# A decoder layer's front stage: the projection on B, C and the step size in two fp32r passes, and another order of the second loop

## What is computed

```
xz = layernorm(x) * gamma + beta  @ W_in          # 256 -> 2 x 512
x_inner, z = split(xz)
x_conv = silu(conv1d(x_inner, conv_w, 4 taps) + conv_b)
xp = x_conv @ W_x                                 # 512 -> 16 (B) + 16 (C) + 1 (step)
Bmat, Cmat, delta = xp[:16], xp[16:32], softplus(xp[32])
h = exp(delta * A) * h + delta * B * x_conv       # along the tokens
y = (sum_n h * C + x_conv * D_skip) * silu(z)
x = layernorm(x + (y @ W_out + x))
```

## Time and profile before

| | us |
|---|---|
| median of 3 runs | 1918.02 (1914.12 to 1920.33) |
| the profiled execution, its own time | 1918.45 |
| its span | 1916.7 |
| TensorE busy in the span | 1763.7 (92%) |
| VectorE, ScalarE, GpSimd busy | 1075.5, 757.1, 709.6 |
| first loop | about 17 to 278 us of the span |
| second loop | about 290 to 558 us |
| the stages behind it (attention, experts) | about 569 us to the end |

### The profile page before, as it was taken

One profiled execution on the slowest core, in us unless ns is written; L12 is line 12 of the kernel. 1 busy time (PEld: TensorE's weight loads), 2 busy tenths in 40 slices (PEclk: granted clock), 3 DMA queues, 4 the chain that ended last, 5 costly groups with the idle time before them and its releaser, 6 DMA issues.

```text
span 1916.7 us, 33397 instructions
## 1 busy us (share of the span) xinstructions
PE 1763.7 (92%) x8984; PEld 1440.8 (75%) x8985; DVE 1075.5 (56%) x2536; ACT 757.1 (40%) x1355; POOL 709.6 (37%) x623
## 2 busy tenths in 40 slices
PE   6999987999947899999999998999999999999980
PEld 4666655888845778888888876888888888888870
DVE  6777767888825567666676773333333333333326
ACT  5777754666512332322323232332333333333326
POOL 1110005898822334534445352332332232232233
PEclk9999998999977899999999999999999999999995
DMA  4444465888624332122221244333333333333329
GB/s 135 171 170 170 170 225 155 244 263 251 234 78 147 101 104 91 69 73 90 79 90 68 76 156 122 54 52 53 52 53 53 51 54 54 51 54 52 52 36 353
DMA packets 137704, 220.63 MB, mean 115 GB/s; under 512 B 40544, under 2 KB 110368, under 8 KB 129328
## 3 DMA queue, kind: packets, MB, share of 16 engines
q1 hardware_dynamic: 112064, 184.44, 29.1%
q0 software_dynamic: 25584, 35.54, 10.8%
HBM read 122.79 MB, written 97.12 MB: 115 GB/s over the span
## 4 chain that ended last, share of the span: by engine, by line
PE 39%; DMA 11%; POOL 6%; issue 6%; DVE 4%; ACT 2%; SPq 1%; POOLq 0%; ACTq 0%; DVEq 0%
PE back_ps L2381 13%; DMA acc<-back_y,back_token 9%; PE back_ps L2401 8%; PE back_ps L2283 5%; POOL back_turned_qk L1663 4%; PE back_ps L2269 3%; POOL sorted L1651 3%; PE back_ps L2260 3%; PE back_ps L2390 2%; PE back_ps L2214 2%; ACT back_out L1816 2%; PE back_ps L2222 2%; DVE back_y L2136 1%; DMA back_c_raw<-in_ctx_T 1%; PE back_ps L2369 1%
## 5 line engine op out<-in xcount | busy, mean ns | idle before, releaser
L2381 PE MATMUL back_ps<-back_w_gu,back_xe_T 128*128 x1620 | 407.6, 400 | 0.3 <-issue 0.2
L1689 POOL DMA_INDIRECT acc<-back_y,back_token x135 | 210.1, 1556 | 499.4 <-DVE back_y L2136 456.0
L2381 PEld LDWEIGHTS back_ps<-back_w_gu,back_xe_T 128*128 128x128 f32 x1620 | 295.4, 189 | 58.7 <-issue 1.0
L2129 DVE TENSOR_TENSOR back_h<-back_silu,back_ps 128x512 f32<-128x512 f32 x135 | 92.7, 687 | 366.9 <-PE back_ps L2381 366.9
L2401 PE MATMUL back_ps<-back_w_down,back_he_T 128*128 x1080 | 255.6, 380 | 0.8 <-ACT back_he_T L1810 0.8
L2401 PEld LDWEIGHTS back_ps<-back_w_down,back_he_T 128*128 128x128 f32 x1080 | 195.1, 191 | 21.6 <-issue 1.0
L1147 PE MATMUL front_ps<-front_xn_T,front_w_in_parts 128*128 128x512 f32 x768 | 186.4, 399 | 5.2 <-issue 3.3
L1651 POOL DMA_INDIRECT sorted<-back_x,back_slot x128 | 133.7, 1044 | 134.8 <-DVE back_slot L1960 100.6
L1147 PEld LDWEIGHTS front_ps<-front_xn_T,front_w_in_parts 128*128 128x128 f32 x768 | 143.3, 190 | 48.3 <-issue 18.5
L993 DVE SCALAR_TENSOR_TENSOR front_conv<-front_ps,front_conv_wb,front_conv 128x508 f32<-128x508 f32 (+2 forms) x192 | 141.2, 742 | 63.3 <-ACT front_conv L829 58.8
L1810 ACT ACTIVATE back_he_T<-back_ps 128x512 f32<-128x512 f32 x135 | 80.7, 598 | 242.4 <-PE back_ps L2390 242.4
(11 more groups left out here) (222 smaller groups left out, 2892.7 us busy)
## 6 DMA issues: line engine op xcount, KB each, us to landing
back_xe<-sorted SPq DMA_DIRECT2D x135, 136.0 KB, 2.1
gate_T<-front_gate_T SPq DMA_DIRECT2D x16, 1024.0 KB, 4.7
xc_T<-front_xc_T SPq DMA_DIRECT2D x16, 1024.0 KB, 5.6
front_xc_in<-xc_T SPq DMA_DIRECT2D x16, 1024.0 KB, 5.4
front_gate_in<-gate_T SPq DMA_DIRECT2D x16, 1024.0 KB, 6.4
front_x_rows<-in_x SPq DMA_DIRECT2D x16, 512.0 KB, 5.4
front_c_rep<-c_parts SPq DMA_DIRECT2D x128, 64.0 KB, 4.5
front_rows_in<-in_x SPq DMA_DIRECT2D x16, 512.0 KB, 7.3
```

The costliest lines, as they stand in the source:

```text
L1689: pool.indirect_dma_start(out=d["acc"][:, :], out_offset=bass.IndirectOffsetOnAxis(ap=token[:, r:r + 1], axis=0), in_=y[:, r % 2], in_offs ...
L2381: op = nc.tensor.matmul(dst[:, r % 2], xe_T[:, r % 2, x_part, k], w_gu[:, bass.ds(e, 1), m, w_part, k], start=(n == 0), stop=(n == len(PAS ...
```

## The change

1. **First loop.** `project_xp` no longer multiplies `w_x` in full fp32. `split_w_x` (VectorE, once) puts high part and rest of `w_x` side by side in `w_x_parts` (97 columns). For each j, ScalarE rounds `xc_T` (`round_xc`), GpSimd takes the rest (`rest_of_xc`), and TensorE multiplies the 97 columns by both parts: two fp32r passes per j, in four places of the body instead of one. The rows 64 to 96 of the result are copied out by ScalarE (`evacuate_xp`, now ahead of `evacuate_turned`) and added by VectorE (`join_xp`, ahead of `split`). `evacuate_xp_rows` comes later.
2. **Between the loops.** The last group's `join_xp` stands inside the first `softplus`; the second `softplus` comes before the second loop; the step sizes too are split into high part and rest (`delta_parts`).
3. **Second loop.** `late` and `early` are two fp32r passes each, on masks made twice (16 small ScalarE instructions a step instead of 8). VectorE: first two skip terms, the statistics of k-2, last two skip terms, then the products. GpSimd: gates in two halves round the norm, `inner` scaled one step ahead (`scale_segment`). ScalarE: first two `dx` ahead of the masks, exp of `inner` one step ahead, at the step's end.

The diff, cut to its core:

```diff
+            def rest_of_xc(g, u, j):
+                pool.wait_ge(xc_high_ready, KI * g + j + 1)
+                nc.gpsimd.tensor_tensor(xc_parts[:, j % 2, 1], xc_T[:, u, j], xc_parts[:, j % 2, 0].bitcast(F32),
+                                        ALU.subtract).then_inc(xc_low_ready, 1)
...
+                    if not is_at(g, 0):
+                        rest_of_xc(g - 1, 1 - u, KI - 1)
+                    rest_of_xc(g, u, 0)
+                    rest_of_xc(g, u, 1)
                     if not last:
-                        rstd_of(2 * pair + u + 2, u)
+                        rstd_of(g + 2, u)
+                    rest_of_xc(g, u, 2)
...
+            def apply_gate(k, u, first):
+                if first == 0:
+                    pool.wait_ge(gate_loaded[u], loads(k, u))
+                for j in (first, first + 1):
+                    pool.wait_ge(skip_added, KI * k + j + 1)
+                    nc.gpsimd.tensor_tensor(y_T[:, u, j], y_T[:, u, j], gate_in[:, u, j], ALU.mult).then_inc(y_ready, 1)
...
+                if there(k):
+                    apply_gate(k, u, 0)
...
+                    apply_gate(k, u, 2)
+                if there(k + 2):
+                    scale_segment(k + 2)
...
+            def round_xc(g, u, j):
+                act.wait_ge(xc_ready, KI * g + j + 1)
+                if not (is_at(g, 0) and j < 2):
+                    act.wait_ge(xp_part_done, KI * g + j - 1)
+                nc.scalar.activation(xc_parts[:, j % 2, 0], xc_T[:, u, j], ACT.Copy).then_inc(xc_high_ready, 1)
+
+            def evacuate_xp(g):
+                act.wait_ge(xp_part_done, KI * (g + 1))
+                if not is_at(g, 0):
+                    act.wait_ge(xp_T_ready, g)
+                nc.scalar.activation(xp_low, ps_xp[XP_LOW:XP_BOTH], ACT.Copy).then_inc(xp_low_ready, 1)
...
                     bias_tap(g, u, 1)
                     silu_conv(g, u, 0)
                     gate(g, u, 1)
+                    round_xc(g, u, 0)
+                    if not is_at(g, 0):
+                        evacuate_xp(g - 1)
                     if ahead:
                         evacuate_turned(g + 1)
-                    if not is_at(g, 0):
-                        evacuate_xp(g - 1, 1 - u)
                     bias_tap(g, u, 2)
                     silu_conv(g, u, 1)
                     gate(g, u, 2)
+                    round_xc(g, u, 1)
+                    bias_tap(g, u, 3)
+                    silu_conv(g, u, 2)
                     if not is_at(g, 0):
                         evacuate_xp_rows(g - 1)
-                    bias_tap(g, u, 3)
-                    silu_conv(g, u, 2)
                     gate(g, u, 3)
+                    round_xc(g, u, 2)
...
+                act.wait_ge(delta_parts_ready, 4 if is_at(g, GROUPS - 1) else 2)
+                act.sem_inc(act_passed, 1)
+                for part in range(2):
+                    for s in range(GS):
+                        step_size = delta_parts[:, part].bitcast(F32)[:, bass.ds(g * GS + s, 1)]
+                        nc.scalar.activation(upto[:, part, s], masks[:, MASK_UPTO], ACT.Copy, scale=step_size
+                                             ).then_inc(upto_ready, 1)
+                        nc.scalar.activation(after[:, part, s], masks[:, MASK_AFTER], ACT.Copy, scale=step_size
+                                             ).then_inc(after_ready, 1)
...
+                    if not early_group(g):
+                        act.wait_ge(y_done, KI * (g - 1))
+                    scale_x(g, ug, 0)
...
+                if there(k + 2):
+                    act.wait_ge(scaled, k + 3)
+                    nc.scalar.activation(inner, inner, ACT.Exp).then_inc(inner_exp, 1)
...
+            def split_w_x():
+                gap = XP_LOW - XP
+                nc.vector.tensor_copy(w_x_parts[:, :, 0:XP], w_x).then_inc(w_x_ready, 1)
+                nc.vector.tensor_copy(w_x_parts[:, :, XP:XP_LOW], w_x[:, :, 0:gap]).then_inc(w_x_ready, 1)
+                dve.wait_ge(w_x_ready, 1)
+                nc.vector.tensor_tensor(w_x_parts[:, :, XP_LOW:], w_x, w_x_parts[:, :, 0:XP].bitcast(F32),
+                                        ALU.subtract).then_inc(w_x_ready, 1)
+
+            def join_xp(g, u):
+                dve.wait_ge(xp_low_ready, g + 1)
+                dve.wait_ge(xp_stored[u], loads(g, u, 32) - 16)
+                if not early_group(g):
+                    dve.wait_ge(xp_turned, g - 1)
+                nc.vector.tensor_tensor(xp_T[:, u], ps_xp[0:XP], xp_low, ALU.add).then_inc(xp_T_ready, 1)
...
                     convolve(g, u, 1)
+                    if not is_at(g, 0):
+                        join_xp(g - 1, 1 - u)
                     if not (last and u):
                         split(g + 1, 1 - u)
...
+                if a == 0:
+                    join_xp(GROUPS - 1, 1)
...
+            softplus(most, SEQS)
+            all_steps(most, SEQS)
             choose()
...
+                    add_skip(k, u, 0)
+                if there(k - 2):
+                    g = k - 2
+                    for s in range(GS):
+                        dve.wait_ge(sum_ready, 2 * g + s // 2 + 1)
+                        nc.vector.bn_stats(stats_1[:, s], sum_rows[:, s]).then_inc(stats_1_ready, 1)
+                    dve.wait_ge(stats_1_ready, GS * (g + 1))
+                    dve.sem_inc(dve_passed, 1)
+                    for s in range(GS):
+                        nc.vector.bn_aggr(mean_1[:, s], stats_1[:, s]).then_inc(mean_1_ready, 1)
+                if there(k):
+                    add_skip(k, u, 2)
...
+            def project_xp(g, j):
+                pe.wait_ge(xc_low_ready, KI * g + j + 1)
+                if is_at(g, 0) and j == 0:
+                    pe.wait_ge(w_x_ready, 3)
+                elif j == 0:
                     pe.wait_ge(xp_T_ready, g)
-                for j in range(KI):
-                    pe.wait_ge(xc_ready, KI * g + j + 1)
-                    op = nc.tensor.matmul(ps_xp, w_x[:, j], xc_T[:, u, j], start=(j == 0), stop=(j == KI - 1))
-                op.then_inc(xp_done, 1)
+                for part in range(2):
+                    op = nc.tensor.matmul(ps_xp, w_x_parts[:, j], xc_parts[:, j % 2, part], start=(j == 0 and part == 0),
+                                          stop=(j == KI - 1 and part == 1))
+                op.then_inc(xp_part_done, 1)
...
                     project(g, u, 0)
+                    if not is_at(g, 0):
+                        project_xp(g - 1, 2)
                     project(g, u, 1)
+                    if not is_at(g, 0):
+                        project_xp(g - 1, 3)
                     if not (last and u):
                         turn(g + 1, 1 - u)
-                    if not is_at(g, 0):
-                        project_xp(g - 1, 1 - u)
                     project(g, u, 2)
-                    if not is_at(g, 0):
-                        turn_xp(g - 1, 1 - u)
-                    project(g, u, 3)
+                    project_xp(g, 0)
+                    project(g, u, 3, None if is_at(g, 0) else lambda: turn_xp(g - 1, 1 - u))
+                    project_xp(g, 1)
...
+                    pe.wait_ge(upto_ready, 2 * GS * (g + 1))
+                    for part in range(2):
+                        op = nc.tensor.matmul(ps_late, mask_ends[:, 0], upto[:, part].rearrange("p s t -> p (s t)"),
+                                              start=(part == 0), stop=(part == 1))
+                    op.then_inc(late_done, 1)
                     if not is_at(g, 0):
                         pe.wait_ge(products_ready, g)
-                    pe.wait_ge(after_ready, GS * (g + 1))
-                    nc.tensor.matmul(ps_early, masks[:, MASK_EARLY], after.rearrange("p s t -> p (s t)"), start=True,
-                                     stop=True).then_inc(early_done, 1)
+                    pe.wait_ge(after_ready, 2 * GS * (g + 1))
+                    for part in range(2):
+                        op = nc.tensor.matmul(ps_early, mask_ends[:, 1], after[:, part].rearrange("p s t -> p (s t)"),
+                                              start=(part == 0), stop=(part == 1))
+                    op.then_inc(early_done, 1)
```

140 lines of the change are left out of this document (69 added, 71 removed).

## The result

The kernel after takes 1923.72 us (median of 20 runs, 1921.07 to 1927.02) where the kernel before takes 1918.69 beside it (20 runs, 1914.12 to 1921.53): a ratio of 1.0029, 95% interval 1.0023 to 1.0035. That is 5 us slower, inside my range of 1893 to 1928, but to the other side of 1918 than my 1915. The execution profiled took 1923.97 us, 5.5 more than the one profiled of before.

A forecast was written before the change was run, and what follows sets the result against it. TensorE was taken to bound both loops before, with rings of waits as the next limits. Terms 5.5 + 1 - 2 - 5.5 - 2 = -3 on 1918.45 us gave 1915 us, range 1893 to 1928.

The forecast's parts named there:

- First loop, +5.5: First loop: thirteen bodies each 0.35 us longer, +4.5, and +1 for split_w_x and the first body's rounding; +2 to +9.
- The ring: First loop: chain of queue orders and waits over ScalarE, VectorE and TensorE, 14.40 us before, 16.5 after, replacing TensorE as limit.
- Rival 1: First loop stays bound by TensorE: a body of 14.5 to 14.8 us, total 1891; chance 0.15.
- Between the loops, +1: Way to the first products: some 6 us added, the last group's softplus steps taken off; +1 us (-1.5 to +3.5).
- Step 0, -2: Second loop's first step: exp of inner ready earlier, interval of 16.2 us becomes about 14; -2 us (-3.5 to 0).
- Steady second loop, -5.5: Second loop: step falls from 14.96 to 14.55 us, 14 intervals x 0.41, -5.5 us (14.15 gives -11, 15.4 gives +6).
- bubble of 1.86 us: Second loop: GpSimd's idle time after scale_segment, ahead of late, 1.86 us a step instead of 1.30.
- rival 2: Second loop: GpSimd's ring with all its standing, 15.4 us a step, total 1928; sign: later skip_added after third gate; chance 0.15.
- two rings: Second loop: GpSimd's ring, 13.4 to 15.4 us a step, and SyncE's, 14.2 to 14.9; 14.55 taken in the middle.
- SyncE's ring: Second loop: load_reps, then the load of xc_in that turn_x needs next step; 14.2 us a step at least, 14.9 with slowest landing.
- Loop end, -2: End of second loop: skip terms ahead of the statistics free the last step's apply sooner; -2 us (-2.5 to 0).
- Rival 3: First loop: rest_of_xc(g, 0) meets the first cast at the shared port, +8 us, total 1923; chance 0.07.

The follow-up runs named there:

- doubled gate: The SiLU of the gate of quarter 3 made twice per first-loop body: in the kernel after 1931.80 us, in the kernel before 1917.64 us.
- last_group_first: Kernel after with project(15, 3) put ahead of project_xp(15, 0) on TensorE in the last group of the first loop: 1919.44 us.
- exp_behind_late: Kernel after with ScalarE's exp of inner put back behind the exps of late and early of its own step: 1909.06 us.
- rounding_early: ring_shorter with ScalarE's rounding of quarter 0 right behind its SiLU, ahead of the affine, and gate 1 behind the affine: 1901.47 us.
- turn_first: Kernel after with turn ahead of project_xp(g-1, 3), the affine ahead of round_xc(g, 0) and evacuate_xp, join_xp behind split: 1933.49 us.
- ring_shorter: turn_first with project_xp(g, 0) between the halves of project(g, 3), plus the orders of exp_behind_late and last_group_first: 1913.24 us.

## Why the prediction went wrong, step by step

- **First loop, +5.5, measured +2.5.** The ring is right and is what bounds the loop (doubled gate). Its length was over-sized by 0.23 us a body: 16.27, not 16.5. The affine came at 5.41 as worked out; the third convolution started 10.3 us after the first bias tap (144.13) where I had 10.4, and `normalise` 1.69 us after SiLU 2 where I had 1.81. My +1 for the first body was +0.6. TensorE stood for 1.26 us of a body (15.00 busy of 16.26), not for some 2. Rival 1 (TensorE bound, 14.5) is out.
- **Between the loops, +1, measured +4.0.** This step failed. From the softplus's start to the first `apply` nothing changed (24.71 us before, 24.57 after), so the eight more masks, `delta_parts` and the join were paid for, as I counted, by the softplus of the last group. The price lies ahead of it, from `silu_conv`(15, 0) to the softplus: 9.34 us before (269.47 to 278.81), 13.45 after (272.02 to 285.47). last_group_first has 11.13 (272.65 to 283.78), so 2.3 of the 4.1 us are what I left out: `project`(15, 3) queued behind a projection that waits for the DMA. I had both halves in hand, the wait of 5.38 us and the new order on TensorE, and asked only which operations were added, not what stood behind the waiting one. The other 1.8 us stay with the mended order. About 1.1 of them lie between the last bias tap and the softplus (6.66 us there, 5.58 before), where ScalarE has two roundings and `evacuate_xp_rows` more; no run takes these out by themselves.
- **Step 0, -2, measured -0.2 to the first `sum_rows`.** The first product of `inner` still stood (L1187 at 315.80, 3.95 us, beside four gates from 313.71 to 318.67; 3.86 in the earlier trace rows), because VectorE comes to it only behind the four skip terms, and from the third of them on GpSimd has gates to run. The interval itself fell from 16.22 to 15.36.
- **Steady second loop, -5.5, measured +3.9.** The step that turned the sign. My bubble of 1.86 us is there (1.76), and TensorE's saving too (14.20 busy instead of 14.84). What failed is "with the norm's steps moved between them, most of that 1.96 may go": it didn't go. The gates got shorter (1765 to 1585 ns each) and so did the scaling of `inner` (2374 to 1961), 1.1 us a step together; 4-column steps of the norm stand in their place (L828 at 1091 ns, 233 before; L829 at 421, 226 before), 1.05 us. With 13.29 of work and 1.74 of bubble in the step shown the ring is near rival 2's, 15.24 instead of 15.4, though not by rival 2's sign: the skip terms of the later half end at 392.38, long before the third gate at 397.70. I had taken a middle value of two rings that do not average: the longer one sets the time, and its lower end was a hope about which instructions meet. exp_behind_late shows what the step is without the bubble's exp: 14.24, near TensorE's 14.15 of my sum. The Trainium skill (SBUF — State Buffer, section "Who interferes with whom") says that whoever issues first holds the shared pair for the whole instruction and that the other one blocks; the 1091 ns of a 4-column step (395.07 to 396.16, while VectorE's product runs from 394.02 to 396.07) and the casts of rounding_early agree.
- SyncE's ring was near, too: between 350 and 515 us of after, `turn_x` waits for the load of `xc_in` in 11 steps, 10.0 us in all, where before has no such wait. In exp_behind_late such waits of matmuls and weight loads together are 3.7 us, against 22.0 in after over the same steps. With the step at 14.24 there it was not the first limit; alone I didn't test it.
- **Loop end, -2, measured -3.5**: right in kind, under-sized.
- **Rival 3** (the port in the first loop) did not show in the kernel after: the rest of quarter 0 ran from 138.68 to 139.97, ahead of the first cast at 140.06. It was 0.1 us away, and in turn_first and ring_shorter, which made the affine earlier and the rest later, it was there at 1.1 us a body.
